# Second cross-attention of a decoder: one copy of the denominators turned, inverted at 32 columns, and laid over the heads by TensorE

## The reference

```python
def _L1_xattn_ref(q, k, v):          # q: norm of x; k and v: ctx_2048
    N_HEAD = 8
    b, d, m = q.shape                # 16, 64, 256
    c = v.shape[1]
    h = N_HEAD
    qh = q.reshape(b * h, d // h, m)
    kh = k.reshape(b * h, d // h, -1)
    vh = v.reshape(b * h, c // h, -1)
    scale = 1.0 / jnp.sqrt(jnp.asarray(d // h, dtype=q.dtype))
    qk = jnp.einsum('bdm,bdn->bmn', qh, kh) * scale
    sm = jax.nn.softmax(qk, axis=-1)
    ret = jnp.einsum('bmn,bcn->bcm', sm, vh)
    return ret.reshape(b, c, m)
...
    x = x + _L1_attn_ref(_layernorm(x, axis=-1), ...)
    x = x + _L1_xattn_ref(_layernorm(x, axis=-1), ctx_2048, ctx_2048)
    x = x + _L1_ffn_ref(_layernorm(x, axis=-1), ...)
```

## Time and profile before

| what | value |
|---|---|
| median of 3 runs | 927.01 us (918.31 to 930.27) |
| the profiled execution | 925.53 us |
| its span, first to last instruction | 923.7 us |
| mean granted TensorE clock | 0.925 |
| TensorE busy (weight loads) | 775.8 us, 84% (483.8) |
| VectorE busy | 546.7 us, 59% |
| ScalarE busy | 336.2 us, 36% |
| GpSimd busy | 255.3 us, 28% |
| the wide reciprocal, L1791 | 8 times, 1748 ns each |

### The profile page before, as it was taken

One profiled execution on the slowest core, in us unless ns is written; L12 is line 12 of the kernel. 1 busy time (PEld: TensorE's weight loads), 2 busy tenths in 40 slices (PEclk: granted clock), 3 DMA queues, 4 the chain that ended last, 5 costly groups with the idle time before them and its releaser, 6 DMA issues. The chain is left out here.

```text
span 923.7 us, 13581 instructions
## 1 busy us (share of the span) xinstructions
PE 775.8 (84%) x4383; PEld 483.8 (52%) x4383; DVE 546.7 (59%) x1333; ACT 336.2 (36%) x774; POOL 255.3 (28%) x316
## 2 busy tenths in 40 slices
PE   4888957999998999997778998899797169999980
PEld 1444536887565666663345555455454136555650
DVE  3789846533332222224889999999964525444545
ACT  1455434332232222212256656666653012222220
POOL 2343420520000000006543344544524202322332
PEclk8999967999999999999899999999986569999995
DMA  9355441390289999818400011110311069999926
GB/s 336 146 223 205 163 157 52 111 367 1 89 299 345 382 318 315 292 57 217 143 1 17 7 36 38 35 41 23 122 74 52 26 221 320 307 323 316 329 90 238
DMA packets 57097, 157.90 MB, mean 171 GB/s; under 512 B 7180, under 2 KB 36748, under 8 KB 51708
## 3 DMA queue, kind: packets, MB, share of 16 engines
q1 hardware_dynamic: 51700, 141.96, 44.1%
q0 software_dynamic: 5328, 15.08, 4.5%
HBM read 114.20 MB, written 42.81 MB: 170 GB/s over the span
## 5 line engine op out<-in xcount | busy, mean ns | idle before, releaser
L1245 PE MATMUL ps<-f_rg,f_xT 128*128 128x512 f32 (+1 forms) x276 | 111.8, 528 | 4.4 <-DMA f_rg<-w_routed 3.8
L1148 DVE TENSOR_TENSOR f_rh<-f_gate,ps 128x256 f32<-128x256 f32 (+1 forms) x69 | 26.0, 377 | 122.7 <-ACT f_gate L977 80.6
L2059 ACT ACTIVATE b_PX<-ps 128x512 f32<-128x512 f32 x128 | 72.8, 597 | 45.1 <-PE ps L2294 43.2
L1784 DVE TENSOR_REDUCE b_smax<-ps 128x4 f32<-128x1024 f32 x64 | 77.7, 1214 | 14.8 <-PE ps L2270 14.8
L2556 POOL DMA_INDIRECT y<-f_ys,f_to x47 | 45.1, 959 | 113.3 <-DVE f_ys L2605 109.9
L1245 PEld LDWEIGHTS ps<-f_rg,f_xT 128*128 128x128 f32 x276 | 52.5, 192 | 32.9 <-issue 23.9
L977 ACT ACTIVATE f_gate<-ps 128x256 f32<-128x256 f32 (+1 forms) x69 | 24.1, 349 | 123.7 <-PE ps L1245 123.2
L2294 PE MATMUL ps<-b_Q,b_Cx 100*128 100x256 f32 x256 | 56.2, 325 | 9.3 <-ACT b_PX L2059 6.7
L1547 POOL MEMSET b_half<- 128x1 f32 x1 | 0.1, 98 | 224.3 <-POOLq L66 224.3
L1268 PE MATMUL ps<-f_rd,f_rhT 128*128 128x256 f32 x230 | 60.9, 380 | 0.3 <-issue 0.3
L2574 ACT ACTIVATE f_gate<-ps 128x224 f32<-128x224 f32 x47 | 16.8, 357 | 113.2 <-PE ps L2652 113.2
(11 more groups left out here) (321 smaller groups left out, 1737.4 us busy)
## 6 DMA issues: line engine op xcount, KB each, us to landing
f_rg<-w_routed SPq DMA_DIRECT2D x23, 1280.0 KB, 7.8
rows<-a_blank SPq DMA_DIRECT2D x16, 1152.0 KB
rw<-w_ffn SPq DMA_DIRECT2D x24, 704.0 KB
f_rw<-w_ffn SPq DMA_DIRECT2D x23, 704.0 KB
f_rd<-w_routed SPq DMA_DIRECT2D x23, 640.0 KB, 5.4
f_xs<-rows SPq DMA_DIRECT2D x47, 144.0 KB
f_yk<-y SPq DMA_DIRECT2D x8, 512.0 KB, 7.1
raw<-w_shared SPq DMA_DIRECT2D x10, 384.0 KB
```

What stands on the lines that cost most here:

```text
L1245: mm = nc.tensor.matmul(ps[:, u % 4, 0:2 * n], xT[b % 2][:, c, :], rg[b % R_SLOTS][:, off:off + 2 * n], start=(c == 0), stop=(c == C - 1))
L1784: nc.vector.tensor_reduce(smax[t % 2][:, k // C, k % C, :], ps[:, FIRST:FIRST + 2, :].rearrange("p u (g n) -> p (u g) n", g=2), AX, ALU.ma ...
L2059: nc.scalar.activation(PX[g % RING][:].rearrange("p c m -> p (c m)"), ps[:, RETS + G_TURN[g] % 2, :], ACT.Exp, scale=XSC).then_inc(turn_re ...
```

## The change

`spread_ret` now lays out the numerators alone (two products, into columns 0 to 255 of the bank). One copy of each denominator is turned: for each half k of the heads and each half c of the 256 columns m, a chunk of `ret` is the stationary operand and 8 columns of the identity move, so that the bank's columns 256 to 287 hold 128 m x 32 (c, k, h, j). VectorE inverts these 32 columns in a step of its own, `denominators`, between `take` and `maxima(b_, 3)`. ScalarE copies the numerators out of the bank (`spread`) and the inverses 8 times side by side (`rwide`), between `x_exp(a_, 1)` and `keep_pT(e_, 1)`. TensorE turns `rwide` back with the identity (`spread_den`), behind `turn_probs(a_, 1)`, into columns 256 to 511. VectorE multiplies and goes on as before.

```diff
-        rden = sb("rden", [P, D])
-        selr = sb("selr", [P, 2, 64])
+        rden = sb("rden", [P, C, 2, 2, G4])
+        rwide = sb("rwide", [P, C, 16, 8])
+        spread = sb("spread", [P, D])
+        selr = sb("selr", [P, 64])
...
+            def denominators(t):
+
+                if t is None:
+                    return
+                dve.wait_ge(den_turned, t + 1)
+                nc.vector.reciprocal(rden[:].rearrange("p c k h j -> p (c k h j)"), ps[:, OUT, D:D + 32]).then_inc(rden_ready, 1)
+
             def add_cross(t):
                 if t is None:
                     return
-                dve.wait_ge(ret_spread, t + 1)
-                step.done(nc.vector.reciprocal(rden[:], ps[:, OUT, D:2 * D]))
-                step.wait()
-                nc.vector.tensor_tensor(crossed[:], ps[:, OUT, 0:D], rden[:], ALU.mult).then_inc(read_cross, 1)
+                dve.wait_ge(ret_kept, t + 1)
+                dve.wait_ge(den_spread, t + 1)
+                nc.vector.tensor_tensor(crossed[:], spread[:], ps[:, OUT, D:2 * D], ALU.mult).then_inc(read_cross, 1)
...
                 take(front(e_))
+                denominators(c_)
...
+            def keep_spread(t):
+                if t is None:
+                    return
+                act.wait_ge(rden_ready, t + 1)
+                if t >= 1:
+                    act.wait_ge(read_cross, t)
+                nc.scalar.copy(spread[:], ps[:, OUT, 0:D])
+                nc.scalar.copy(rwide[:], bc(rden[:].rearrange("p c k h j -> p (c k h j)"), 3, 8)).then_inc(ret_kept, 1)
...
                 x_exp(a_, 1)
+                keep_spread(b_)
                 keep_pT(e_, 1)
...
                 pe.wait_ge(ret_ready, t + 1)
-                for q in range(2):
+                for k in range(2):
+                    mm = nc.tensor.matmul(ps[64 * k:64 * k + 64, OUT, 0:D], selr[:], ret[:, k],
+                                          start=True, stop=True, tile_position=(0, 64 * k))
+                one = ident.rearrange("p (j h x) -> p h j x", j=G4, h=2)[:, :, :, 8]
+                for c in range(C):
                     for k in range(2):
-                        mm = nc.tensor.matmul(ps[64 * k:64 * k + 64, OUT, q * D:(q + 1) * D], selr[:, q], ret[:, k],
-                                              start=True, stop=True, tile_position=(0, 64 * k))
-                mm.then_inc(ret_spread, 1)
+                        at = D + c * 16 + k * 8
+                        mm = nc.tensor.matmul(ps[:, OUT, at:at + 8].rearrange("p (h j) -> p h j", h=2), ret[:, k, c * P:(c + 1) * P], one,
+                                              start=True, stop=True)
+                mm.then_inc(den_turned, 1)
+
+            def spread_den(t):
+
+                if t is None:
+                    return
+                pe.wait_ge(ret_kept, t + 1)
+                for c in range(C):
+                    mm = nc.tensor.matmul(ps[:, OUT, D + c * P:D + (c + 1) * P],
+                                          rwide[:, c].rearrange("p g r -> p (g r)"), ident, start=True, stop=True)
+                mm.then_inc(den_spread, 1)
...
                 turn_probs(a_, 1)
+                spread_den(c_)
                 turn_max(b_, 1)
```

More of the change, by code:

```diff
@@ L1472, in attention1 @@
         ret_ready = sem("ret_ready")
-        ret_spread = sem("ret_spread")
+        den_turned = sem("den_turned")
+        rden_ready = sem("rden_ready")
+        den_spread = sem("den_spread")
+        ret_kept = sem("ret_kept")
         logits_ready = sem("logits_ready")
@@ L1666, in set_selectors @@
                 nc.vector.tensor_copy(upper[:], KR[:, R_UP:R_UP + P])
-                for q in range(2):
-                    ins = nc.vector.tensor_copy(selr[:, q].rearrange("p (h j r) -> p h j r", h=2, j=G4),
-                                                ident.rearrange("p (j h q r) -> p q h j r", j=G4, h=2, q=2)[:, q])
-                ins.then_inc(selr_set, 1)
+                nc.vector.tensor_copy(selr[:].rearrange("p (h j r) -> p h j r", h=2, j=G4),
+                                      ident.rearrange("p (j h q r) -> p q h j r", j=G4, h=2, q=2)[:, 0]).then_inc(selr_set, 1)
             def add_rows(t):
@@ L2066, in keep_ret @@
                 nc.scalar.copy(ret[:], ps[:, OUT, :].rearrange("p (k m) -> p k m", k=2)).then_inc(ret_ready, 1)
+            def keep_spread(t):
[5 more added lines that the diff above has]
+                nc.scalar.copy(spread[:], ps[:, OUT, 0:D])
+                nc.scalar.copy(rwide[:], bc(rden[:].rearrange("p c k h j -> p c (k h j)"), 3, 8)).then_inc(ret_kept, 1)
             def exp_logits(t):
@@ L2326, in spread_ret @@
                 pe.wait_ge(ret_ready, t + 1)
-                for q in range(2):
-                    for k in range(2):
-                        mm = nc.tensor.matmul(ps[64 * k:64 * k + 64, OUT, q * D:(q + 1) * D], selr[:, q], ret[:, k],
-                                              start=True, stop=True, tile_position=(0, 64 * k))
-                mm.then_inc(ret_spread, 1)
+                for k in range(2):
[3 more added lines that the diff above has]
+                for c in range(C):
+                    for k in range(2):
+                        at = D + c * 16 + k * 8
[10 more added lines that the diff above has]
+                mm.then_inc(den_spread, 1)
             def count_in_front(t, at):
```

## The result

The changed kernel took 935.57 us (median of 4 runs, 930.34 to 940.51) against 928.62 us before (4 runs): 1.0100 times as long, with an interval of 1.0053 to 1.0147. So it is slower, by 7 to 12 us, and within the 2% that were named beforehand.

The account below looks back on a forecast made before the run. VectorE sets the pace, but leads the POOL and TensorE strand into `add_attention` by only 0.24 us. Terms 2.8 + 2.6 + 0.7 + 1.5 = 7.6 us on the profiled 925.53 gave 933 us, range 923 to 941.

Parts of the forecast that it names:

- the 2% that were named beforehand: Whole time: a measurement tells about 2%; chance 0.96 within it, 0.03 slower by 2%, 0.01 faster by 2%.
- VectorE's saving would be spent waiting: VectorE before `add_attention`: ready after the product at 635.2, it then waits 1.1 us for the output projection.
- the eight small records: TensorE's `spread_ret`: four added products of 8 columns take 1.04 us by their weight loads, 1.2 at most.
- VectorE's wait before `add_attention`: Sign of being right: VectorE idle about 1 us there in every round, with the projection named as releaser.
- the 32.6 named as a sign: Sign of being right: rounds of 32 us grown to about 32.6.
- Tiles 1 to 4: Rounds of these tiles: `add_attention` 0.7 us later each, 2.8 us in all (ends 0.35 and 1.1 a tile).
- Part 5: TensorE: `spread_den` takes 0.60 us, the steps queued behind it start 1.03 later, the projection ends 0.88 later.
- Tiles 0 and 5: Rounds without the 0.24 us in hand: 1.3 us more each, 2.6 us in all (0.8 to 1.8).
- Tile 6: Cross-attention on the way to the routing: longer latency from `ret` to the product, 0.7 us more (0 to 1.2).
- Tile 7: Last tile, alone at half clock: `ret` to product 5.2 us against 3.8, put at 1.5 us (1.2 to 1.8).
- The list of what is queued behind a new wait: VectorE at the small reciprocal, tiles 5 and 6: maximum 3 waits up to 1 us, TensorE's later scores behind it.
- The clock: Rival: half clock covers `spread_ret` to the projection, 4.5 us a tile; 942 us for two tiles, 946.5 for three; chance 0.10.

Follow-up runs that it names:

- again: The changed kernel once more, unaltered, beside the kernel before on one chip: 928.59 against 916.78 us, 1.0125 times the kernel before.
- short_recip: The kernel before with the reciprocal over 32 of 256 denominator columns, leaving out the others (wrong values): 0.9966 times the kernel before.
- two_more: The kernel before with two idle products on TensorE where the change puts `spread_den`: 0.9997 times the kernel before.
- two_copies: The kernel before with two 128x256 copies on ScalarE where the change puts its own: 1.0024 times the kernel before.
- one_small: The changed kernel with one of the four small products that turn the denominators (partly wrong denominators): 1.0029 times the kernel before.
- before_filled: The kernel before with `first_scores` 8 and 9 ahead on TensorE and `maxima(b_, 4)` ahead of `add_cross` on VectorE: 1.025 times the kernel before.

## Why the prediction was right, and where it was not

933 us was forecast and 935.6 measured, within 2% as nearly all of the chance had it, and slower, as forecast. That the sum came so near is partly luck: its terms for the steady rounds were too high, its term for the last tile was too low, and some 5 us of `again`'s loss are in no term. The argument that VectorE's saving would be spent waiting held: short_recip gives 1.11 us back of 1.40. The sizes of the new pieces held too: the reciprocal 0.35 us (0.35 forecast), the eight small records 1.06 (1.04), `spread_den` 0.65 to the next step (0.60), VectorE's wait before `add_attention` about 1 us forecast and 0.74 measured. The rounds of 32.2 to 32.5 us look like the 32.6 named as a sign, but they owe it to half-clock stretches; at full clock it is 31.65 against 31.38.

Term by term:

- *Tiles 1 to 4, 0.7 us each.* Measured 0.27 at full clock. The step that failed is in Part 5: the start of the queue behind `spread_den`, 1.03 us later, was carried over to the projection as 0.88, while the trace has it 0.40 later (2.99 against 2.59). Its premise was that TensorE's work in between has no other wait, as in "the low end is the bare product without any wait for ScalarE: 0.60 - 0.24 = 0.35 us late". two_more shows that the bare product costs nothing, because the 2.59 us to the projection ran through ScalarE's queue and not through TensorE's. The rows for it were there: the values end at 633.54, `keep_aT` starts 0.40 us later and ends at 634.31, and the projection starts at 634.37. I followed the order on TensorE and not what it waited for.
- *Tiles 0 and 5, 1.3 us each.* Tile 0's round took 1.3 us more (31.29 against 30.03); tile 5's, against two_copies, 0.8.
- *Tile 6, 0.7 us.* The stretch to tile 7's `ret` is at half clock for a quarter to nearly a half of its length, and went from 43 to 50 us over the profiles of kernels that do not differ there. This term can't be told from it.
- *Tile 7, 1.5 us.* From `ret` to the product 1.59 measured (6.05 less 4.46). Behind it, 2.5 us more that the prediction did not have. The list of what is queued behind a new wait was made for the steady rounds, with maximum 3 alone; in the last round it is `take_slots`, and through it GpSimd's scatter.
- *The clock.* It was given a chance of 0.10, in one form: on the strand from `spread_ret` to the projection. The half-clock stretch comes elsewhere, behind TensorE's wait half way through the round. The named pieces, 1.9 for the rounds to tile 5's, 1.3 for tile 0's, 1.6 and 2.5 for tile 7, make some 7 us of the 12 measured beside `again`. Over that comparison's runs the mean granted clock was 0.929 in the changed kernel and 0.937 in the kernel before. That this makes the other 5 us fits, and so does one_small, which has the clock of the kernel before and is only 3 us slower. It was not shown: no run here changes the clock and nothing else.

## What to carry to other kernels

When an engine is full, look for the second-longest strand into each instruction that reads another engine's result, before shortening the engine's work: 0.24 us of lead there was the measure of the gain (0.20 a full round in short_recip), and not the 1.75 us of the instruction. Follow that strand by what each step waits for; a step on an engine's stream whose result another engine picks up late is free, as in two_more, and it need not stay so once it is chained behind two others. Read the first and the last round of a pipeline by themselves: a new wait that is covered in the middle stands at the end in front of work that had been hidden in it.

## What the runs showed of the hardware that was not expected

A product of 8 columns with a new 128x128 float32 stationary operand takes about as long as its two weight loads, 0.13 us a record at full clock and 0.24 at half (8 in 1.06 and in 1.88 us). Some 2 us without work on TensorE were followed by a granted clock of 0.50 for over 3 us in the changed kernel and for over 8 us in before_filled, whose rounds grew by 6 us; the same instructions in a slightly different order were 2.5% slower. In the kernel before, a wait as long was followed by a fall at 591 us and by none at 623 us. The reciprocal on VectorE takes 6.2 ns a column (0.35 us for 32, 1.75 for 256), while a product of 256 columns takes 0.42 us in all.
